# First message stage of a graph network: products of two groups summed together in four strips, waits left out, index columns fetched by another queue

## What is computed

```python
xs = concat([x[src, :8], x[dst, :8]])
xv = concat([x[src, 8:].reshape(E, 8, 3), x[dst, 8:].reshape(E, 8, 3)])
h = 2**0.5 * relu(emb @ W1 / 10**0.5)
w = (h @ W2 / 16**0.5).reshape(E, 7, 16, 8)
s_out = PW_S * (einsum('eu,euw->ew', xs, wa_s) + INV3 * einsum('eui,ei,euw->ew', xv, y1, wb_s))
g_out = PW_S * (einsum('eu,euw->ew', xs, wa_g) + INV3 * einsum('eui,ei,euw->ew', xv, y1, wb_g))
v_out = PW_V * (...)                                  # three more sums over u, with wc, wd, we
edge_ftr = concat([1.593 * tanh(s_out), 1.593 * tanh(g_out)[:, :, None] * v_out]) * norm
out = segment_sum(edge_ftr, dst)
```

## Time and profile before

| | us |
|---|---|
| median of 3 runs (lowest, highest) | 5658.57 (5657.39, 5661.72) |
| the profiled execution, its own time | 5663.47 |
| its span, from the first to the last instruction | 5661.7 |
| PE busy | 4006.7 (71%) |
| DVE busy | 3192.8 (56%) |
| POOL busy | 3379.2 (60%) |
| ACT busy | 1475.9 (26%) |
| the first message stage: first product on DVE at 428.27, last one from 3349.61 on for 3.61 | 2924.95 |

### The profile page before, as it was taken

One profiled execution on the slowest core, in us unless ns is written; L12 is line 12 of the kernel. 1 busy time (PEld: TensorE's weight loads), 2 busy tenths in 40 slices (PEclk: granted clock), 3 DMA queues, 4 the chain that ended last, 5 costly groups with the idle time before them and its releaser, 6 DMA issues. The chain is left out here.

```text
span 5661.7 us, 70210 instructions
## 1 busy us (share of the span) xinstructions
PE 4006.7 (71%) x20839; PEld 2129.7 (38%) x20839; DVE 3192.8 (56%) x5351; ACT 1475.9 (26%) x2862; POOL 3379.2 (60%) x3371
## 2 busy tenths in 40 slices
PE   0005888787888888877877860099898998999870
PEld 0002322222222222232222320077666666766650
DVE  4504776776767776677776763044444444455442
ACT  2002444444444444444444430000000000001000
POOL 5675555555555555555555417666666666666756
PEclk9999888888888888888888985599999989999985
DMA  8411111111111111111111101022222222222211
GB/s 300 114 38 18 38 37 36 37 37 37 37 35 33 36 37 31 34 37 37 37 37 37 35 18 22 18 41 45 43 43 43 42 43 43 43 42 48 46 27 24
DMA packets 266652, 252.42 MB, mean 45 GB/s; under 512 B 182208, under 2 KB 236936, under 8 KB 263777
## 3 DMA queue, kind: packets, MB, share of 16 engines
q1 hardware_dynamic: 157028, 174.83, 11.2%
q0 software_dynamic: 109024, 72.30, 9.0%
q10 hardware_dynamic: 462, 4.00, 0.2%
HBM read 160.54 MB, written 90.34 MB: 44 GB/s over the span
## 5 line engine op out<-in xcount | busy, mean ns | idle before, releaser
L612 POOL DMA_INDIRECT edge<-xp_d,idx x1440 | 1421.4, 987 | 1089.0 <-issue 419.4
L864 DVE TENSOR_TENSOR prod<-G_ps,hid 128x1000 f32<-128x1000 f32 x1200 | 1399.4, 1194 | 884.6 <-remote 410.6
L1198 POOL DMA_INDIRECT gxb<-tab_d,idxb x1200 | 1259.1, 1049 | 577.0 <-issue 334.4
L753 PE MATMUL G_ps<-FT,wst 32*128 32x500 f32 x4800 | 999.3, 685 | 362.7 <-DVE prod L864 244.4
L1233 PE MATMUL G_ps<-tb,hot 125*126 125x500 f32 (+1 forms) x3200 | 727.8, 378 | 395.5 <-DVE hotk L1255 301.1
L782 PE MATMUL R_ps<-prod,red 128*32 128x500 f32 x4800 | 923.8, 706 | 0.8 <-ACT rt L678 0.8
L1233 PEld LDWEIGHTS G_ps<-tb,hot 125*126 125x126 f32 x3200 | 572.0, 201 | 537.5 <-issue 446.8
L753 PEld LDWEIGHTS G_ps<-FT,wst 32*128 32x128 f32 x4800 | 270.7, 200 | 827.5 <-DVE prod L864 412.3
L773 PE MATMUL T_ps<-FT,wst 32*128 32x500 f32 x800 | 522.4, 737 | 3.1 <-issue 3.1
L666 ACT ACTIVATE FT<-T_ps 128x500 f32<-128x500 f32 x400 | 235.0, 588 | 856.3 <-PE G_ps L753 629.9
L782 PEld LDWEIGHTS R_ps<-prod,red 128*32 128x32 f32 x4800 | 180.8, 124 | 691.2 <-issue 445.5
(11 more groups left out here) (242 smaller groups left out, 4541.3 us busy)
## 6 DMA issues: line engine op xcount, KB each, us to landing
xd_d<-zeros SPq DMA_DIRECT2D x16, 1562.5 KB
y_d<-zrb SPq DMA_DIRECT2D x40, 595.0 KB
edge<-xp_d,idx POOLq DMA_INDIRECT x1440
xv<-xd_d SPq DMA_DIRECT2D x40, 560.0 KB
y_d<-zr SPq DMA_DIRECT2D x40, 560.0 KB
edge<-sel_d SPq DMA_DIRECT2D x40, 546.9 KB
gxb<-tab_d,idxb POOLq DMA_INDIRECT x1200
em<-in_edge_attr SPq DMA_DIRECT2D x40, 175.0 KB
```

Of the source, the lines that this page charges most:

```text
L612: nc.gpsimd.indirect_dma_start(out=edge_c[:, i, 8:8 + DIM], out_offset=None, in_=xp_d, in_offset=bass.IndirectOffsetOnAxis(col, 0)).then_i ...
L753: return Tn.matmul(G_ps[pair][:, a * 512:a * 512 + GW], wst[rows, r * 128:(r + 1) * 128], FT[k][rows, :], start=True, stop=True)
L864: V.tensor_tensor(prod[k][i][:, :].rearrange("p (a e) -> p a e", a=2), gv, hid[k][:, :].rearrange("p (a e) -> p a e", a=1).broadcast_to([1 ...
L1198: nc.gpsimd.indirect_dma_start(out=gx[h][:, c * T1:(c + 1) * T1], out_offset=None, in_=tab_d, in_offset=bass.IndirectOffsetOnAxis(idx[h][: ...
```

## The change

**Sums (PE).** `reduce`, for one group, becomes `sum_round`, for a piece of two groups: four matmuls side by side in four strips of `R_ps`, in three rounds (u = 0, 1, 2). Strips 0 and 1 take the first group, strips 2 and 3 the second. Rounds 0 and 2 stand behind `round1` of the next piece's two groups, round 1 behind `hidden`. `back` is called once a piece, on 128 rows, behind `hidden` of the second group. `prod` gets four sets of buffers in place of two, `rt` one tile of 128 rows in place of two of 96, `red` a third block, and `Y_ps` is laid out with 64 columns for each column of edges.

**ACT and DVE.** `out_of_R` runs once a piece. `tanh`, `high` and `out_of_R` stand first in a group, `relu` ahead of `out_of_T`. `turned` and `along` move from the first group of a pair to the second and are one group earlier in effect, `post` 0 and 1 move the other way and are one group later. `sums` moves by one group in the chunk. Waits that another wait covers are dropped.

**Index columns.** POOL's copy goes; SP brings 40 columns from `src` in DRAM for each chunk (two DMAs), behind the store of the chunk before, after waiting for the gathers that last read `idx`. POOL waits for `b_ix`.

```diff
-            prod = [[sbt(f"prod{k}_{i}", [128, 2 * GW]) for i in range(3)] for k in range(2)]
-            rt = [sbt(f"rt{k}", [96, GW]) for k in range(2)]
+            prod = [[sbt(f"prod{k}_{i}", [128, 2 * GW]) for i in range(3)] for k in range(4)]
+            rt = sbt("rt", [128, GW])
...
+                    def load_index(t, h):
+                        if not isinstance(t, int):
+                            for s in range(h * PC, h * PC + PC):
+                                hold(S(f"b_gx{s}"), t * 16 * PW + 32 * PW)
+                        by_rows(sp, idx[0:P, h * C:(h + 1) * C], edges(src, 1)[:, bass.ds((t * 2 + h + 4) * C, C)], S(f"b_ix{h}"))
...
-                                if c == 0 and s % PC == 0 and not fixed:
-                                    for q in range(s, s + PC):
-                                        hold(S(f"b_gx{q}"), t * 16 * PW + 16 * PW)
-                                    nc.gpsimd.tensor_copy(idx[:, i:i + C], src_i[:, bass.ds((p + RING) * PW, C)]).then_inc(S("b_ix"), 1)
-                                    hold(S("b_ix"), t * 2 + s // PC - 1)
+                                if i % C == 0 and not fixed:
+                                    hold(S(f"b_ix{i // C}"), t * 32)
...
                         for g in range(G2):
-                            if k == 1 and not (last and g + 3 >= G2):
-                                s = (g + 3) // 2
+                            if k == 0 and not (first and g < 4):
+                                tanh(t * RING + g // 2 - 2)
+                            if k == 0 and not (last and g + 4 >= G2):
+                                s = (g + 4) // 2
                                 high(t * RING + s, s % RING, t * 2 + s // PC)
+                            if k == 1 and not (first and g < 2):
+                                out_of_R(t * RING + g // 2 - 1)
...
-                    def reduce(n, k):
-                        pe.wait_ge(S("b_mul"), n * 3 + 3)
-                        if some(n):
-                            pe.wait_ge(S("b_rt"), n)
-                        for a in range(2):
-                            for o in range(3):
-                                i = (o, (0, 2, 1)[o])[a]
-                                last = Tn.matmul(R_ps[32 * o:32 * o + 32, 0:GW], red[:, a * KF:(a + 1) * KF], prod[k][i][:, a * GW:(a + 1) * GW], start=(a == 0), stop=(a == 1))
-                        last.then_inc(S("b_R"), 1)
+                    def sum_round(m, b, u):
+                        if u == 0:
+                            pe.wait_ge(S("b_mul"), m * 6 + 6)
+                            if some(m):
+                                pe.wait_ge(S("b_rt"), m)
+                        for q in range(4):
+                            pair, a = ((0, 0), (1, 0), (2, 0), (0, 1), (2, 1), (1, 1))[q % 2 * 3 + u]
+                            last = Tn.matmul(R_ps[32 * q:32 * q + 32, 0:GW], red[:, u * KF:(u + 1) * KF],
+                                             prod[b * 2 + q // 2][pair][:, a * GW:(a + 1) * GW], start=(u == 0), stop=(u == 2))
+                        if u == 2:
+                            last.then_inc(S("b_R"), 1)
+
+                    def back(m):
+                        pe.wait_ge(S("b_rt"), m + 1)
+                        if some(m):
+                            pe.wait_ge(S("b_yr"), m)
+                        pe.sem_inc(S("go"), 1)
+                        for c in range(GT):
+                            last = Tn.transpose(Y_ps[0:P, c * 128:(c + 1) * 128], rt[:, c * P:(c + 1) * P], ident[:, :])
+                        last.then_inc(S("b_Y"), 1)
...
                             round1(n, k)
+                            if sums_due:
+                                sum_round(m, b, 2 * k)
                             if not (last and g >= G2 - 2):
                                 transposes(n + 2, g2, p2)
-                            if not (first and g < 2):
-                                back(n - 2, k)
                             round2(n, k)
                             if not (last and g == G2 - 1):
                                 hidden(n + 1, 1 - k)
-                            if not (first and g == 0):
-                                reduce(n - 1, 1 - k)
+                            if sums_due and k == 0:
+                                sum_round(m, b, 1)
+                            if sums_due and k == 1:
+                                back(m)
```

More of the change, by code:

```diff
@@ L104, in gnn_resnorm_kernel @@
         wst = sb("wst", [128, NR * 128])
[L105 removed]
+        red = sb("red", [128, 3 * 32])
         attn_b = sb("attn_b", [P, 2 * DIM])
@@ L249, in _ @@
                     nc.gpsimd.memset(edge_c[:, :, SD + 40:EW], 0.0)
-                    for i in range(2):
+                    for i in range(3):
                         blk = red[:, i * KF + i * MO:i * KF + (i + 1) * MO]
@@ L577, in _ @@
                         load_post(h, h, 0)
-                    turn(0, first=True)
-                    with sp.Fori(1, PAIRS - 1) as t:
-                        turn(t)
+                    sp.wait_ge(S("b_idxz"), 1)
+                    turn(0, first=True, index=True)
+                    with sp.Fori(1, PAIRS - 2) as t:
+                        turn(t, index=True)
+                    turn(PAIRS - 2)
                     turn(PAIRS - 1, last=True)
@@ L648, in gather_sums @@
                         act.wait_ge(S(f"b_z{h}"), t * NPC + i + 1)
-                        if some(ch):
+                        if i == 0 and some(ch):
                             act.wait_ge(S("b_st"), ch * 32)
@@ L816, in _ @@
                     turn(PAIRS - 1, last=True)
-                    reduce(NG - 1, 1)
-                    back(NG - 2, 0)
-                    back(NG - 1, 1)
+                    for u in range(3):
+                        sum_round(NPIECES - 1, 1, u)
+                    back(NPIECES - 1)
                 @block.vector
@@ L914, in turn @@
                                 scan = lambda: fill(gc, ch + 1, 1 - h)
-                            if 4 <= gc < 8 and not (first and h == 0):
-                                scan = lambda: sums(gc - 4, ch - 1, 1 - h)
-                            multiply(n, k, 0)
-                            multiply(n, k, 1)
-                            if k == 0 and not (first and g < 4):
-                                q = (g - 4) // 2
+                            if 5 <= gc < 9 and not (first and h == 0):
+                                scan = lambda: sums(gc - 5, ch - 1, 1 - h)
+                            multiply(n, k, b, 0)
+                            multiply(n, k, b, 1)
+                            if k == 1 and not (first and g < 5):
+                                q = (g - 5) // 2
                                 post(2, t * RING + q, q % RING // PC, q % RING % PC, t if q >= 0 else t - 1)
@@ L923, in turn @@
                                 carry_x(ch + 1, 1 - h)
-                            if gc == 3 and not (first and h == 0):
+                            if gc == 4 and not (first and h == 0):
                                 carry_sums(ch - 1, 1 - h, t - 1 + h)
-                            if k == 1 and scan:
+                            if k == 0 and scan:
                                 scan()
-                            multiply(n, k, 2)
-                            if k == 0:
-                                q = (g + 4) // 2
+                            multiply(n, k, b, 2)
+                            if k == 1:
+                                q = (g + 5) // 2
                                 more = not (last and q >= RING)
@@ L937, in turn @@
                                     along(t * RING + q, q % RING)
-                            elif not (first and g < 3):
-                                q = (g - 3) // 2
+                            elif not (first and g < 4):
+                                q = (g - 4) // 2
                                 for i in range(2):
@@ L951, in _ @@
                         fill(i, 0, 0)
-                    for p in range(2):
+                    for p in range(3):
                         turned(p, p, 0, 0, 0)
@@ L958, in _ @@
                     turn(PAIRS - 1, last=True)
-                    post(2, NPIECES - 2, 1, PC - 2, PAIRS - 1)
-                    for i in range(3):
-                        post(i, NPIECES - 1, 1, PC - 1, PAIRS - 1)
+                    for p in range(2):
+                        for i in range(3):
+                            post(i, NPIECES - 2 + p, 1, PC - 2 + p, PAIRS - 1)
                     carry_sums(NCH - 1, 1, PAIRS - 1)
```

89 lines of the change are left out of this document (40 added, 49 removed).

## The result

| | us |
|---|---|
| changed kernel, median of 4 runs (lowest, highest) | 5985.3 (5974.87, 6014.03) |
| kernel before, median of 4 runs beside it | 5660.15 |
| ratio, 95% interval | 1.058 (1.054 to 1.062) |
| profiled execution of the changed kernel, its own time (span) | 5983.25 (5981.5) |

What follows compares the result with a forecast made beforehand. PE was taken to set the pace at half clock, with DVE nearly full at full clock. Clean pace 2132 us with 22.7% lost gave a stage of 2758, 155 less, plus 4 elsewhere: 5508 us, range 5370 to 5650.

Steps and rivals of the forecast that it cites:

- The rest: Work on ACT, POOL and SP beside the sum: expected to stay hidden; extra pieces and a block of red cost 4 us.
- the sum: First message stage: clean pace plus time lost in disturbed stretches gives 2758 us, 155 less.
- the share of time disturbed: First message stage: kept as before the change; the lost share falls from 25.7% to 22.7% through less PE work.
- B: Sums on PE: the four strips don't overlap, a round takes twice as long, 6000 us; chance 0.04.
- clean pace: First message stage undisturbed: 400 groups at 5.33 us, 2132 us, where 5.41 a group gave 2164.
- the clean gain: Undisturbed groups at full clock: of PE's gain of 0.9 us only 0.08 a group comes through, as DVE is late next.
- At half clock: PE at 1.2 GHz: 17.4 us a piece, 8.7 a group in place of 9.7, with PE alone setting the pace.
- A: First message stage: a less busy PE loses its clock more often, granted clock under 0.84, 5948 us; chance 0.12.
- a stretch of 93% busy: PE between falls: busy 93% before the clock falls, held against low activity as the whole cause.
- C: First message stage: late results are waits unrelated to PE work and don't shrink, 5570 us; chance 0.17.
- D: First message stage: less matrix work means fewer falls of the clock, 19% lost, 5382 us; chance 0.08.

Runs made afterwards that it cites:

- e1: Kernel before without the 1440 gathers of the loop, waits for them left at their first targets: 4975 us against 5591 for the kernel before.
- e2: Changed kernel without the gathers of the loop, index columns copied by POOL: 4881 us against 5591 for the kernel before.
- e3: Changed kernel with two gathers each let go behind the 1st, 3rd, 4th and 6th multiply of a piece: 5409 us against 5591 for the kernel before.
- e4: Kernel before with no hold behind post, gathers 3 to 8 of a piece let go together behind the third multiply: 6064 us against 5591.
- f1: Kernel before with two gathers each behind the 1st, 3rd, 4th and 6th multiply of a piece: median 5615.31 us, 0.990 of the kernel before.
- f2: Changed kernel with two gathers each behind the 1st, 3rd, 4th and 6th multiply of a piece, four runs: median 5465.78 us, 0.965 of the kernel before.
- b1: Kernel before with the second of the two rounds of reduce left out, sums incomplete: 5539 us against 5610.
- c1: Changed kernel with the fourth strip used only in round 1 of the sums, two of twelve sum matmuls left out: 5740 us against 5619 for the kernel before.
- c4: Kernel before with reduce moved from the end of the group to directly behind round1: 5748 us against 5619.
- c2: Changed kernel with round 0 of the sums moved to the end of the even group, ahead of round 1: 6156 us against 5619 for the kernel before.
- b2: Kernel before with the index columns brought by SyncE's queue and nothing else of the change: 5499 us against 5610.
- d3: Changed kernel with the index columns copied by GpSimd as before, nothing brought by SyncE: 5952 us against 5662 for the kernel before.

## Why the prediction was wrong

**The step that failed** is in *The rest*: "the gathers that wait for `post` now leave a group later. This hides as long as the mean pace stays over 10.2." It asked whether POOL can keep up, and it can. It didn't ask what a later opening of one hold does to the order in which the holds open: two of the three stopped to hold, and a spread of small runs became one run of eight, 180 of them with 180 falls. In the sum itself stood a second assumption: "I take the share of time disturbed as it is". That share was taken for a property of the chip and of PE's load; e1 and e2 show that nearly all of it belongs to the gathers, and e3 and e4 that the way they are spaced sets how large it is. `pace` itself was not in the diff.

**The sum, point by point.** The rows of PE were read rightly: a round of sums takes 0.98 us to the next block, switch included (0.91 forecast, and 0.2 a piece for the switches, a term for which the prediction has no row); four strips run at the pace of three, so B was no case. Without gathers the stage of the changed kernel takes 2170 us (clean pace 2132 forecast), but that of the kernel before takes 2261 where the sum had 2164: the clean gain is 91 us and not 32. At half clock the sum is at odds with its own rows. `round1` twice 2.10, three rounds of 1.75, transposes twice 0.98, `round2` with `hidden` twice 2.04 and `back` 1.2 make 16.7 us a piece, not 17.4; with 8.35 us a group in place of 8.7 it would have forecast a gain of some 210 us.

With the same holds on both sides the change gains 149.5 us; the forecast had 155. The direction of the gain was right, and so was its rough size. That the numbers lie so close is luck in part: 91 us of the gain are there with no disturbance at all, and the falls, which the sum held as they were, differ between f1 and f2 (134 and 120). b1, which takes 0.9 us of PE work a group away in the order of before, gained only 71 us. The loss of some 520 us between f2 and the changed kernel is the term that was missing.

**The rivals.** A gave 5948 us and the time came to 5985, with a granted clock of 0.81, under the 0.84 named as its sign. Yet its reason fell: a less busy PE keeps its clock for 2000 us when nothing gathers (e2, 85% busy), and b1 with less PE work got faster. That its time came so close to the measured one is luck. The rule of the Trainium skill cited for it ("TensorE: Matmul & The Clock Gate", on the HAM clock gate) has the clock low unless activity releases it. The traces agree as far as the falls go, since they come out of stalls (PE busy for 0.23 in the 3.4 us before a fall). The prediction held against that rule a stretch of 93% busy, but between that stretch and the fall stand 3.40 us with PE busy for 0.76. What the rule doesn't tell is why PE stalls, and that is where the two kernels differ. C took the late results for waits that don't shrink with PE work. They go with the gathers, but not with them alone: from 700 to 3300 us DVE has 657.9 us of "remote" waits in the changed kernel and 523.5 in c1, with less PE work and the same runs of eight. D, fewer falls, is nearest to what an even pace does, from another cause. That the gathers had a part could be suspected from the trace of before: in its stretch from 3240 to 3345 us, behind the last gather, all engines read:

```profile
3240.00:3345.00 105.00, 96.88 (x654) 38.29 (x650) 94.27 (x146) 52.80 (x108) 0.00 (x0) 1.00 0.04 9
```

105 us at 1.00 with POOL at 0, against 0.87 for the stage as a whole. Looking for where a disturbance is absent would have raised the question before the change ran.

## What to carry to other kernels

When some instructions are held back by counters of another engine's work, moving that work by one step changes the holds though no line of theirs is edited: write down in which order the holds open, before and after. A share of time lost to "the clock" can change with the kernel, as it did here; look for a stretch that doesn't lose it, see what is missing there, and then take that away by experiment, since other traces may show the loss without it (c4 here). When a gain worked out from rows turns into a loss of twice its size, measure the change and its side effect apart, since the change may be sound: here two holds of pacing turned 5.8% slower into 3.5% faster.

## What the runs showed of the hardware

- Indirect gathers issued by GpSimd in runs of eight, 1.25 us apart, go with one fall of TensorE's granted clock for each run: 180 falls for 180 runs in the changed kernel, about 10.4 us behind the start of a run, and 94% of these falls come out of 3.4 us in which PE was busy for less than half. Without gathers there are 16 falls in the stage (e1) or none (e2); with two at a time let go, most runs being of two to six, 107 to 134.
- Why gathers go with stalls of PE isn't settled. POOL's issue, the gathers' own DMA traffic and the power that all of it draws go together in every run here. No run had gathers issued while nothing was moved, or the same bytes moved by another queue. Nor was the length of a run told apart from its place among the matmuls: e3 and e4 change both. c1, which leaves out two of twelve sum matmuls under the same 180 runs, had 138 falls, so the work on PE has a part in it; how large a part stays open.
- Falls come without gathers too, where PE has to wait: seven in the last 158 us of the stage in c4.
- What c2 showed, 1.095 of the kernel before where the changed kernel has 1.058, for one round of sums in another place (granted clock 0.75), isn't explained; its runs of eight are those of the changed kernel, and its falls are longer, 8.6 us in the mean against 6.1.
- PE's results come late while the clock is still recorded as full: 0.41 us of PE work in 3.40 us at a recorded 1.00, then 0.58. In such a stretch the granted clock of the record says less than the waits do.
- Bringing the index columns by SP made the kernel before 111 us faster in one run (b2, 104 falls where it has 124) and did nothing for the changed kernel that one run shows (d3). b2's runs of gathers were longer and shorter in other places; I can't say which of them made the difference.
